# Late maxima units placed behind a step's first projection: an attention and expert kernel on one core

## What is computed

```python
x = x + _layernorm(attention(_layernorm(x), Wq, bq, Wk, bk, Wv, bv))
x = x + _layernorm(ffn(_layernorm(x), ...))
# attention, for an inner block: softmax over the blocks it meets
aw = jax.nn.softmax(band, axis=-1)
# ffn: a dense branch and the two best of eight experts
abel_out = _gelu(xn @ abel_w + abel_b)
h = _gelu(einsum('bsd,edh->ebsh', xn, ew1) + eb1[:, None, None, :])
moe_out = moe_out @ expm(gens[i])        # three times
mixed = abel_out * (1.0 - gate) + moe_out * gate
```

## Time and profile before

| what | value |
|---|---|
| median of 3 runs | 1735.96 us (1733.33 to 1737.49) |
| the profiled execution's own time | 1736.45 us |
| its span, first to last instruction | 1734.6 us |
| TensorE busy | 1510.2 us, 87% |
| VectorE busy | 1223.9 us, 71% |
| ScalarE busy | 897.3 us, 52% |
| maxima reductions L1307 | 1024, 500.2 us |
| maxima matmuls L844 | 1280, 267.3 us |

### The profile page before, as it was taken

How to read it: one execution, slowest core, us unless ns; L and a number is a source line. 1 busy time by engine, 2 the same in 40 slices (tenths; PEclk the granted TensorE clock), 3 DMA queues, 4 the chain that set the end, 5 groups by cost and what they waited for, 6 DMA issues and landing times. The chain is left out here.

```text
span 1734.6 us, 33286 instructions
## 1 busy us (share of the span) xinstructions
PE 1510.2 (87%) x10277; PEld 1051.6 (61%) x10342; DVE 1223.9 (71%) x3687; ACT 897.3 (52%) x1782; POOL 696.9 (40%) x705
## 2 busy tenths in 40 slices
PE   7989989989998998899899898799999999999500
PEld 5755455545555554555555466688888888888400
DVE  5677797888888888878887846355556666555297
ACT  3156766676676667667766763233333333333244
POOL 1011324443453344334434434144444444445378
PEclk9999999999999999999999999899999999999855
DMA  8132245335434533553454339556565656555397
GB/s 223 51 123 84 86 145 165 117 119 180 143 113 154 172 120 113 178 158 108 138 162 135 131 112 274 140 97 150 105 150 104 153 104 138 118 133 93 60 323 232
DMA packets 186076, 243.04 MB, mean 140 GB/s; under 512 B 23576, under 2 KB 156576, under 8 KB 185824
## 3 DMA queue, kind: packets, MB, share of 16 engines
q1 hardware_dynamic: 159360, 205.40, 37.7%
q0 software_dynamic: 26592, 36.07, 12.5%
HBM read 133.12 MB, written 105.64 MB: 138 GB/s over the span
## 5 line engine op out<-in xcount | busy, mean ns | idle before, releaser
L1101 ACT ACTIVATE pexp<-scT 128x512 f32<-128x512 f32 x768 | 436.3, 598 | 241.6 <-PE scT L867 211.3
L1307 DVE TENSOR_REDUCE mx<-work 128x1 f32<-128x320 f32 (+2 forms) x1024 | 500.2, 546 | 50.9 <-PE work L844 50.2
L1867 POOL DMA_INDIRECT y_rows<-rows_add,row_of x142 | 224.0, 1578 | 289.7 <-DMA y_rows<-rows_add,row_of 224.0
L867 PE MATMUL scT<-w 128*128 128x192 bf16 (+3 forms) x1472 | 261.4, 270 | 37.6 <-ACT pexp L1101 33.2
L844 PE MATMUL work<-w 126*128 126x320 bf16 (+4 forms) x1280 | 267.3, 295 | 25.3 <-DVE mx L1307 20.2
L1899 PE MATMUL h_ps<-inT,w1c 128*128 128x256 f32 x1136 | 259.1, 381 | 2.4 <-DVE inT L1951 2.4
L1912 PE MATMUL o_ps<-w,hT 128*128 x1136 | 256.8, 379 | 0.0
L1842 ACT ACTIVATE rows_add<-rows_out,row_share 128x257 f32<-128x257 f32 x142 | 64.6, 503 | 350.4 <-DVE rows_out L1967 295.5
L1899 PEld LDWEIGHTS h_ps<-inT,w1c 128*128 128x128 f32 x1136 | 217.1, 191 | 33.0 <-issue 2.9
L867 PEld LDWEIGHTS scT<-w 128*128 128x128 bf16 x1536 | 123.2, 97 | 175.8 <-ACT pexp L1101 116.2
L1912 PEld LDWEIGHTS o_ps<-w,hT 128*128 128x128 f32 x1136 | 210.5, 190 | 25.8
(11 more groups left out here) (200 smaller groups left out, 2067.4 us busy)
## 6 DMA issues: line engine op xcount, KB each, us to landing
w<-split_spill SPq DMA_DIRECT2D x384, 128.0 KB, 2.9
split_spill<-split SPq DMA_DIRECT2D x64, 384.0 KB, 3.2
rows_in<-z_rows SPq DMA_DIRECT2D x71, 265.0 KB, 4.6
y_rows<-pre SPq DMA_DIRECT2D x16, 514.0 KB, 5.8
y<-y_rows SPq DMA_DIRECT2D x16, 514.0 KB, 6.8
x_rows<-x SPq DMA_DIRECT2D x16, 512.0 KB, 2.6
abel_rows<-pre SPq DMA_DIRECT2D x16, 512.0 KB, 3.7
abel_in<-abel_rows SPq DMA_DIRECT2D x16, 512.0 KB, 4.5
```

Of the source, the lines that this page charges most:

```text
L867: ins = nc.tensor.matmul(scT[n % 2][:, at:at + hi - lo], tile(kst[par][0:K_EXP, h, :], t), qst[par][0:K_EXP, h, lo:hi], start=True, stop=True)
L1101: nc.scalar.activation(pexp[:, (q * GROUP + n) % NPB, :], scT[n % 2][:, :], ACT.Exp, scale=DH ** -0.5).then_inc(s_exp, 1)
L1307: emptied(nc.vector.reduce_max(mx[:, c:c + 1], bank(s, "max", b, h, t)[:, 0:n], AX_X), s, "max", b, h, t)
L1867: pool.indirect_dma_start(kept.y_rows, bass.IndirectOffsetOnAxis(ap=row_of[n][:, r:r + 1], axis=0), rows_add[n % 2][:, r, :], None, comput ...
```

## The change

Two places change in a table, and one call moves in VectorE's program. Of the four units of head 12, the first two now stand behind the last score of the last quad, with the turned maxima ahead of them (they stood behind the second and the third score). The other two go from there to the place behind the next step's first projection, where (13,0) already stood. VectorE reduces these three before its part of the first projection and not after it.

```diff
-LATE_AT = [("end", 1), ("end", 2), ("end", 3), ("end", 3),
-           ("proj", 0), ("proj", 1), ("proj", 2), ("proj", 3),
+LATE_AT = [("end", 3), ("end", 3), ("proj", 0), ("proj", 0), ("proj", 0),
+           ("proj", 1), ("proj", 2), ("proj", 3),
...
+                behind("proj", 0)
                 for m in range(4):
 
                     if proj:
                         parts(s, m)
                     if finish and m % 2:
                         finish_a(s - 2, m // 2)
-                    behind("proj", m)
+                    if m:
+                        behind("proj", m)
```

## The result

The changed kernel takes 1742.47 us (median of 6 runs, 1740.05 to 1743.18) against 1734.03 us of the kernel before in 6 runs beside it. The ratio is 1.0045, 95% interval 1.0033 to 1.0057: slower by 0.45%, which is 7.8 us of 1734 (the two medians lie 8.4 apart). In a later group of runs it was 1.0037 (1.0025 to 1.0049). The forecast was +7.1 us, 1743.0 us.

What follows compares the result with a forecast made beforehand. At the seams between steps, TensorE's third projection waits for VectorE's L1291 to empty a bank, behind ScalarE's chain. Terms 6.0 + 1.3 + 0 - 0.24 = +7.1 us gave 1743.0 us, 0.4% slower; range 1738 to 1748.

Steps and rivals of the forecast that it cites:

- (d): Work-bank rotation at 12 seams: first turned output inherits the wait for L1291; 0.50 us net each, 6.0 us.
- the lower bound: At the 12 seams, the inheriting output's weight load hidden by being done beforehand: 0.31 us each, 3.7 us.
- (a): End of the last quad: two units moved behind the fourth score, last exponentials earlier; gain 0.24 us per seam.
- (b): Behind the first projection: two more units push the second projection by 0.30 us; nothing is late through this alone.
- (c): VectorE's three reductions before L1291 fit its idle time under the Gelu and table loads; cost zero, margin 0.3 us.
- (e): Seams into steps 2 and 3, without Gelu: idle time too narrow, third projection 0.6 to 0.7 us later, 1.3 together.
- (f): Seam into step 1: 0, bounds -0.5 and +0.5 us; seam at 984, without projection: -0.24 us.
- Rival A: Rotation covers the evacuation, only the gain at the quad's end remains: faster by 3.6 us, 1732.4 us; chance 0.07.
- Rival B: The 0.74 us rotation loss is taken up by some 0.5 per seam: 1736 to 1738 us; chance 0.15.
- Rival C: Quad-end gain fails and reductions pass their 0.3 us margin by 0.2: 13.1 us slower, 1749 us; chance 0.10.

Runs made afterwards that it cites:

- banks_swapped: Changed kernel, every engine's program in the same order, only the banks of the first turned attention output and third projection exchanged; 1733.32 us, 0.9994 to the kernel before.
- proj_only: Changed kernel with the first two head-12 units put back behind the second and third score; ratio to the kernel before 1.0040, step 60.61 us.
- end_only: Kernel before with all four head-12 units behind the last score of the last quad, (13,0) alone behind the first projection; ratio to the kernel before 1.0013.
- parts_first: Changed kernel without the moved VectorE call: its part of the first projection first, then the three reductions; ratio to the kernel before 1.0048.
- group 3: Later group of runs, on chip number 14, comparing four kernels with the kernel before; the kernel before, repeated there, had ratio 1.0002.
- after_again: Changed kernel, unchanged, run and profiled again in the third group; ratio to the kernel before 1.0037, step 60.49 us.
- before_again: Kernel before, unchanged, run and profiled again in the third group; ratio to itself 1.0002, step 59.93 us.
- before_rotated: Kernel before with only (13,0) reduced ahead of L1291 and banks chosen so (13,2) takes over the first projection's bank; 1731.35 us, 0.9960 to the kernel before.
- four_behind_p0: Changed kernel with one head-12 unit at the end of the step and four units behind the first projection; ratio to the kernel before 1.0288.
- four_end_rotated: All four head-12 units behind the last score, (13,0) alone behind the first projection, reduced ahead of L1291, banks permuted; ratio to the kernel before 0.9956.
- four_end_again: The kernel of four_end_rotated, run again in the third group; 1730.62 us, ratio to the kernel before 0.9957, step 59.16 us.

## Why the prediction was right

1. **(d), the rotation: right, and it is the whole loss of the 12 seams.** C0 inherits the wait, and banks_swapped shows that nothing else does it. The size was put at 0.74 lost per seam; proj_only measured 0.67. The term that was too large is the way from L1291 to P2: 0.91 in the sum (0.06 + 0.19 + 0.66), 0.84 in the trace (L1291 ends 511.75, C0 at 511.90, P2 at 512.59). C0 starts 0.15 behind L1291's end and not 0.25, and P2 0.69 behind C0 and not 0.66. The mis-sized piece is the 0.19 for the weight load. In the rows it was read from (508.24 to 508.43) C0's matmuls had P1 ahead of them until 508.43, so that distance was no price of a load. TensorE's weight loads of the changed kernel show the price:

```profile
511.87 0.42 PEld L895 LDWEIGHTS work<-ident_sb,ctxT 128*128 128x128 f32 x4 [1.62 <-issue]
```

   The load starts 0.12 behind L1291's end (511.75) and the matmul 0.03 behind the load. The Trainium skill, "TensorE: Matmul & The Clock Gate", section "Step-by-step: what each phase is for", says that weight loads are pulled ahead of matmuls in flight. Where C0 waited for no bank the trace agrees (its load at 508.24, with P1 running up to 508.43). Across the wait for the bank it shows no such thing: the load starts behind the release. The prediction was right not to take the lower bound, and wrong to add the whole load.

2. **(a), the end of the quad: right in kind, mis-sized.** 0.24 was taken, 0.14 measured (end_only; also ScalarE's wait, 0.87 to 0.73). I took the unit's whole pitch as won. But the attention product now starts 0.32 us behind the score ahead of it (503.04 to 503.36), where the unit had started 0.23 behind it (500.71 to 500.94): a product starts 0.09 later behind a score than a unit does. The two errors of 1 and 2 nearly cancel: forecast 0.50 per seam, measured 0.53.

3. **(b) and (c): right.** P1 comes 0.30 later behind P0 (2.26 against 1.96), and nothing waits for that: in banks_swapped, with the same 2.26, P2 is at 4.87. The three reductions lie in ScalarE's cover: 509.13 to 510.48, L1291 at 511.00. parts_first confirms that at these seams this side of L1291 is the cheap one.

4. **(e), the seams without a Gelu: right.** The steps from 2 to 3 and from 3 to 4 grow by 0.54 and 0.57, forecast 0.6 to 0.7 each with (a)'s gain in it, bounds 0.4 and 0.9. Two errors cancel here too: within the seam P2 comes 0.70 later behind P0 (4.33 to 5.03) and not 0.92, and (a) gives 0.14 and not 0.24.

5. **(f): right as far as it can be told.** The start of step 1 was put at 0. P0 there comes 0.98 us earlier (counted from L750) but the step behind it is 0.71 longer, together -0.27, inside the bounds of 0.5. That is luck of one pair as much as anything: in group 3 the same step is 2.1 us longer in after_again than in before_again. At the seam into step 16 C0 comes 0.54 later behind P0 of step 15 (0.55 in group 3): the loss of the seam into step 15, less the 0.14 of (a), where (f) had 0.24. The last turns of step 16 come 0.47 later behind that C0 (57.88 us before, 58.35 after), but in group 3 it is 0.30 earlier (58.20 and 57.90), so this isn't the change's. TensorE runs below its upper clock there in both kernels, granted 0.57 and 0.62 in the 4 us behind C0.

6. **The rivals.** Rival A (the rotation covers the evacuation) is excluded by banks_swapped, and more: the rotation did not even cover it before. Rival B (the delay is taken up) is excluded by the step length. Rival C's failing margin in (c) did not happen.

What I did not see in the kernel before is what before_rotated showed: I read the 0.76 us wait of P2 as the mark of a path set by ScalarE, and forecast with it, without asking what the path would be if another use took the bank.

## What to carry to other kernels

When work is moved among uses that share buffers in rotation, write out the rotation before and after, and for each long-held buffer name who comes N uses later; the moved work costs what that successor's wait costs, not its own duration. Do it on both sides: for the uses behind the moved ones and for the moved ones' own successors, and give long-held buffers to work that comes late in the program. A gap on one engine that can be filled for free says nothing about the engine whose order must change to fill it.

## What the runs showed of the hardware

- A wait of 2.27 us on TensorE, behind a stretch of short units, was followed at 9 of 14 seams by matmuls at the lower clock level, and at 5 by none (four_behind_p0). Where it was, at the seam shown, the projection took 3.16 us instead of 1.82, granted clock 0.58. In end_only 1.83 us ahead of P0 in step 1 were followed by the same, P0 taking 3.16 us with the granted clock at 0.50 (windows of end_only, columns as above):

```profile
100.00:102.00 2.00, 1.07 (x2) 0.64 (x3) 0.92 (x4) 0.00 (x0) 0.00 (x0) 0.83 0.00 0
102.00:104.00 2.00, 2.00 (x3) 0.49 (x2) 0.00 (x0) 0.00 (x0) 0.00 (x0) 0.50 0.06 12
```

  The wait of 0.82 us at the seam into step 8 of the changed kernel left the clock at 1.00 (506 to 514 us). So the two long waits shown cost about 1.3 us each (3.16 - 1.82) beyond their own length.
- Two groups of runs on the same chip, 1 and 2, differ by 0.37 us in the time from a score to its exponential at one place of the steps with a Gelu (0.43 and 0.80), and the kernel before by 9 us in its median (1734.39 and 1743.33). The ratio of four_end_rotated held across groups 2 and 3 (0.9956, 0.9957); its step length did not.
- In step 1 a maxima unit waits for the DMA that restacks the projections, for a time that differs between executions (1.5 us in before_again, 1.3 in four_end_again, 2.2 in before_rotated, 0.7 in the first profile of the kernel before), so the first steps scatter more than the change moves them.
